# Three of the seven layer-0 chunks computed as three rounded passes, and layer-0 work placed sooner in a group

## What is computed

```
x = x0
for k in (k0, k1, k2):
    x = jnp.einsum('bhd,bmd,ohm->bod', x, x0, k)
    outputs.append(jnp.sum(x, axis=-1))
```

## Time and profile before

| what | value |
|---|---|
| median of 3 runs | 709.17 us |
| profiled execution | 707.73 us, span of its instructions 705.9 us |
| first group's first matmul | 38.57 us |
| last group's first matmul | 602.08 us |
| end of the last group's layer-1 matmuls | 636.02 us |
| distance between the first matmuls of two neighbouring groups | 36.86 us for the first, then 37.61 to 37.63 us |
| TensorE / VectorE / ScalarE / GpSimd busy, share of the span | 93% / 82% / 78% / 48% |
| mean granted TensorE clock | 0.985 of full speed |

### The profile page before, as it was taken

One profiled execution on the slowest core, in us unless ns is written; L12 is line 12 of the kernel. 1 busy time (PEld: TensorE's weight loads), 2 busy tenths in 40 slices (PEclk: granted clock), 3 DMA queues, 4 the chain that ended last, 5 costly groups with the idle time before them and its releaser, 6 DMA issues.

```text
span 705.9 us, 10117 instructions
## 1 busy us (share of the span) xinstructions
PE 658.9 (93%) x2528; PEld 467.6 (66%) x2528; DVE 581.7 (82%) x1316; ACT 550.7 (78%) x1957; POOL 336.5 (48%) x351
## 2 busy tenths in 40 slices
PE   0799999999999999999999999999999999997998
PEld 0367676767677777767676767676777777672583
DVE  0568989898998989898989898988989898997390
ACT  1268888888888888888888888888888888995393
POOL 6665747556474737373837465564737330000000
PEclk9999999999999999999999999999999999996799
DMA  6530712030303030302112030303030300200000
GB/s 211 129 115 11 262 25 101 11 114 7 118 5 120 4 116 8 97 28 70 55 40 84 11 113 11 114 6 119 5 120 4 115 7 1 78 1 0 0 1 0
DMA packets 56666, 43.04 MB, mean 61 GB/s; under 512 B 37007, under 2 KB 40335, under 8 KB 56352
## 3 DMA queue, kind: packets, MB, share of 16 engines
q1 hardware_dynamic: 50090, 40.28, 18.3%
q0 software_dynamic: 5120, 1.32, 1.9%
q10 hardware_dynamic: 1398, 0.80, 0.4%
HBM read 40.41 MB, written 1.97 MB: 60 GB/s over the span
## 4 chain that ended last, share of the span: by engine, by line
PE 74%; DVE 12%; ACT 8%; issue 2%; DMA 2%; POOL 1%; SPq 0%; ACTq 0%; DVEq 0%
PE Y L437 16%; PE Y L435 16%; PE Y L436 16%; PE X L392 13%; ACT Y L265 6%; DVE chain L338 5%; PE GB L401 4%; DVE chain L332 3%; DVE z L305 1%; PE X L466 1%; PE X L464 1%; PE X L465 1%; PE X L388 1%; POOL x0g L184 1%; ACT x1hi L229 1%
## 5 line engine op out<-in xcount | busy, mean ns | idle before, releaser
L265 ACT ACTIVATE Y<-Y,xtok 128x128 f32<-128x128 f32 x1536 | 420.6, 382 | 56.0 <-PE Y L437 56.0
L435 PE MATMUL Y<-k1lo,x1hi 128*128 128x512 f32 x640 | 305.9, 478 | 10.8 <-DVE x1lo L302 10.4
L338 DVE TENSOR_TENSOR chain<-chain,Y 128x512 f32<-128x512 f32 x384 | 263.6, 686 | 49.9 <-ACT Y L265 40.9
L437 PE MATMUL Y<-k1hi,x1lo 128*128 128x512 f32 x640 | 251.8, 393 | 0.0
L436 PE MATMUL Y<-k1hi,x1hi 128*128 128x512 f32 x640 | 250.7, 392 | 0.0
L184 POOL DMA_INDIRECT x0g<-in_table,rows_now x160 | 153.9, 962 | 42.1 <-issue 37.2
L435 PEld LDWEIGHTS Y<-k1lo,x1hi 128*128 128x128 f32 x640 | 120.3, 188 | 65.5 <-DVE x1lo L302 17.7
L205 POOL TENSOR_TENSOR diag<-xtok,mask 128x320 f32<-128x320 f32 x64 | 47.3, 740 | 230.0 <-PE GB L401 214.5
L436 PEld LDWEIGHTS Y<-k1hi,x1hi 128*128 128x128 f32 x640 | 120.7, 189 | 46.1 <-issue 21.6
L197 POOL TENSOR_TENSOR pairs<-pairs,A 120x512 f32<-120x512 f32 x105 | 133.0, 1290 | 13.6 <-DMA pairs<-scratch 12.6
L437 PEld LDWEIGHTS Y<-k1hi,x1lo 128*128 128x128 f32 x640 | 120.2, 188 | 26.2
(11 more groups left out here) (52 smaller groups left out, 262.4 us busy)
## 6 DMA issues: line engine op xcount, KB each, us to landing
pairs<-scratch SPq DMA_DIRECT2D x109, 240.0 KB
A<-scratch SPq DMA_DIRECT2D x16, 240.0 KB
k1raw<-in_k SPq DMA_DIRECT2D x1, 2560.0 KB, 9.9
x0g<-in_table,rows_now POOLq DMA_INDIRECT x160, 2.3
k2s<-in_k SPq DMA_DIRECT2D x1, 2560.0 KB, 14.2
scratch<-x0g SPq DMA_DIRECT2D x93, 20.0 KB, 1.7
pairs<-in_w SPq DMA_DIRECT2D x3, 256.0 KB, 3.0
pairs<-scratch ACTq DMA_DIRECT2D x3, 240.0 KB
```

What stands on the lines that cost most here:

```text
L265: ins = nc.scalar.activation(first[:, o] if c == 0 else y[:, o], y[:, o], ACT.Copy, scale=xtok[g % 2][:, j, m:m + 1])
L338: nc.vector.tensor_tensor(chain[:, :], chain[:, :], Y[(NCH * T + c) % YB][:, :], ALU.add).then_inc(s_chain, 1)
L435: nc.tensor.matmul(y, hi[:, tok], k1lo[:, cols], start=True, stop=False)
L437: nc.tensor.matmul(y, lo[:, tok], k1hi[:, cols], start=False, stop=True).then_inc(s_y, 1)
```

## The change

Chunks 4, 5 and 6 of layer 0 are no longer one f32 matmul each but three `f32r` passes: low weights by high products, high by high, high by low. For it ScalarE writes the high part of each product (`high_product`, a copy into the new tile `pairs_hi`), and GpSimd the low part, in place of the product (`low_product`, a subtraction). ScalarE does chunk 4's, 5's and 6's high part after its own work at p = 16, 18 and 24; GpSimd does the three low parts in tile 2, behind product 6 and ahead of that tile's four gathers. The weights are split once at the start. The matmuls of layer 0 stand at p = 5, 8, 12, 17, 23, 26, 29 in place of 5, 9, 14, 18, 22, 27, 31; `x1_high` at p = 30 in place of 33; the transposes at p = 2 in place of 1. VectorE does `x1_low` and `z0_sums` earlier in its last tile.

```diff
-XTOK_PE_AT, XTOK_AT = 1, 3
-L0_AT = (5, 9, 14, 18, 22, 27, 31)
-X1HI_AT = 33
+XTOK_PE_AT, XTOK_AT = 2, 3
+L0_AT = (5, 8, 12, 17, 23, 26, 29)
+SPLIT = (4, 5, 6)
+HIGH_AT = (16, 18, 24)
+X1HI_AT = 30
+LOWS_OF_TILE = ((), (), SPLIT, ())
...
+            def low_product(g, c):
+                pool.wait_ge(s_ph, len(SPLIT) * (g - 1) + SPLIT.index(c) + 1)
+                nc.gpsimd.tensor_tensor(pairs_lo[c][0:PR, :], pairs[c][0:PR, :], pairs_hi[c][0:PR, :].bitcast(f32),
+                                        ALU.subtract).then_inc(s_pl, 1)
...
                         for c in PRODUCTS_OF_TILE[j]:
                             product(g + 1, c)
+                        for c in LOWS_OF_TILE[j]:
+                            low_product(g + 1, c)
                     if g + 2 < NG:
                         gather(g % 2, range(*GATHERS_OF_TILE[j]))
...
+            def high_product(g, c):
+                act.wait_ge(s_prod, NC0 * (g - 1) + c + 1)
+                act.wait_ge(s_l0, NC0 * (g - 1) + c + 1)
+                nc.scalar.activation(pairs_hi[c][0:PR, :], pairs[c][0:PR, :], ACT.Copy).then_inc(s_ph, 1)
...
+                        elif p in HIGH_AT:
+                            high_product(g + 1, SPLIT[HIGH_AT.index(p)])
...
+            act.wait_ge(s_w0sum, 1)
+            nc.scalar.activation(w0hi[:, :], w0[:, SPLIT[0] * O:], ACT.Copy).then_inc(s_w0hi, 1)
...
+            dve.wait_ge(s_w0hi, 1)
+            nc.vector.tensor_tensor(w0lo[:, :], w0[:, SPLIT[0] * O:], w0hi[:, :].bitcast(f32),
+                                    ALU.subtract).then_inc(s_w0lo, 1)
...
                 add_scaled(T, 1)
+                if j == TPG - 1 and g + 1 < NG:
+                    x1_low(g + 1)
...
                 mac(T, 6)
                 if j == TPG - 1 and g + 1 < NG:
-                    x1_low(g + 1)
+                    z0_sums(g + 1)
...
                 add_scaled(T, 7)
-                if j == TPG - 1 and g + 1 < NG:
-                    z0_sums(g + 1)
...
+            def layer0_split(c):
+                i = SPLIT.index(c)
+                w, hi, lo = slice(i * O, (i + 1) * O), pairs_hi[c][0:PR, :], pairs_lo[c][0:PR, :]
+                nc.tensor.matmul(X1[:, :], w0lo[:, w], hi, start=False, stop=False)
+                nc.tensor.matmul(X1[:, :], w0hi[:, w], hi, start=False, stop=False)
+                nc.tensor.matmul(X1[:, :], w0hi[:, w], lo, start=False, stop=(c == NC0 - 1)).then_inc(s_l0, 1)
...
+                            if c0 in SPLIT:
+                                pe.wait_ge(s_w0lo, 1)
+                                pe.wait_ge(s_pl, len(SPLIT) * g + SPLIT.index(c0) + 1)
+                                layer0_split(c0)
+                            else:
+                                pe.wait_ge(s_prod, NC0 * g + c0 + 1)
+                                layer0(c0)
```

More of the change, by code:

```diff
@@ L70, in build @@
         pairs = [sb(f"pairs{i}", [P, GROUP]) for i in range(NC0)]
+        pairs_hi = {c: sb(f"pairs_hi{c}", [P, GROUP], f32r) for c in SPLIT}
+        pairs_lo = {c: over(f"pairs{c}", f"pairs_lo{c}", [P, GROUP], f32r) for c in SPLIT}
         x1hi = [sb(f"x1hi{i}", [P, GROUP], f32r) for i in range(2)]
@@ L83, in build @@
         w0 = sb("w0", [PR, NC0 * O])
+        w0hi = sb("w0hi", [PR, len(SPLIT) * O], f32r)
+        w0lo = sb("w0lo", [PR, len(SPLIT) * O], f32r)
         w2s = sb("w2s", [P, H1 // P, H2])
@@ L113, in build @@
         s_roll = [sem(f"rolled_in{i}") for i in range(NC0)]
+        s_w0hi, s_w0lo, s_ph, s_pl = [sem(n) for n in (
+            "w0hi_ready", "w0lo_ready", "high_products_ready", "low_products_ready")]
         s_first, s_prod, s_l0 = sem("first_products_ready"), sem("products_ready"), sem("l0_done")
@@ L445, in _ @@
                                 pe.wait_ge(s_xtok, g + 2)
-                            pe.wait_ge(s_prod, NC0 * g + L0_AT.index(p) + 1)
-                            layer0(L0_AT.index(p))
+                            c0 = L0_AT.index(p)
+                            if c0 in SPLIT:
[5 more added lines that the diff above has]
+                                layer0(c0)
                     if c == G_AT and T > 0:
```

## The result

The changed kernel takes 731.59 us, the median of 5 runs (725.5 to 735.96), against 708.82 for the kernel before: a ratio of 1.0328, with an interval of 1.0279 to 1.0378. It is slower by 3.3%. The forecast was 731, with 712 to 749 for 8 in 10. The profile is of the fastest of the five, 725.5 us.

A forecast was written before the change was run, and what follows sets the result against it. TensorE, busy 93%, was taken to bound the old kernel, VectorE 4 us behind. Fourteen turns of a new 39.3 us loop start the last group at 624.0, span 728.3, giving 731 us; 712 to 749 for 8 in 10.

The forecast's parts named there:

- The passes save 0.18 each: TensorE, layer 0: three passes at 0.687 us replace an f32 matmul at 0.87, saving 0.55 us per group over three chunks.
- The boundary waits go, a wait for VectorE comes, 36.8 per group without the loop: Group start: 1.38 us of TensorE waits vanish, VectorE's late reduction adds 1.1 to 35.7, giving 36.8 us per group.
- tile 3 has no layer-0 matmul: VectorE's last tile: without layer-0 work there, TensorE reaches the next `make_G` at p = 4 before VectorE delivers the reduction.
- GpSimd's low parts cost 1.27: GpSimd: three subtractions shaped like a product, 1.27 us each (bounds 1.0 and 1.6), 3.8 us more per group.
- The gathers wait for ScalarE's high part, and a loop of 39.3 us closes: GpSimd, tile 2: gathers behind `low_product` 6 wait for ScalarE behind p = 24; first product to first product takes 39.3 us.
- From the issue of the load of `A3` to the first product, 5.4: Last term of the loop: from SyncE issuing the `A3` load to the next group's first GpSimd product, 5.4 us.
- the lower bound of 4.15: Same loop term at its shortest: `A3` and the first roll, 481 KB, moved 4.15 us after the issue; loop 38.0 us.
- Waits of about 2 at the transposes and 1 at chunk 4: Sign in the profile: TensorE waits about 2 us at the transposes for `A3`, about 1 at chunk 4's passes for GpSimd.
- The sum: First product at 41.31, fourteen turns of 39.3, last group at 624.0, span 728.3: 731 us.
- The clock falls: Rival: TensorE's waits near each group's start drop the clock to 1.2 GHz; 748 us, longer stretches more; chance 0.08.
- Faster: Rival: the loop never decides, TensorE and VectorE set 36.8 us per group; 697 us, chance 0.12.
- the shorter loop: Rival: DMAs seen complete nearly with their last byte and a light subtraction, loop 38.0 us; about 713 us, chance 0.12.

The follow-up runs named there:

- e12: Kernel before with only the split of chunks 4 to 6, low parts spread, other TensorE and VectorE steps at their old places: 702.43 us, ratio 0.9902.
- e5: Changed kernel with high copies after p = 11, 16, 20 and the low parts spread over tiles 1 and 2: 700.29 us, ratio 0.9896 to the kernel before.
- e9: Changed kernel with spread low parts, earlier high copies, layer 0's last two chunks after p = 28 and 31, X1 copy after 32: 692.24 us.
- e6: Changed kernel with spread low parts, earlier high copies, only layer 0's last chunk moved to p = 31, X1 copy after 32: 700.02 us.
- e1: Changed kernel with the low parts of chunks 5 and 6 behind tile 2's four gathers, chunk 4's ahead: 707.37 us, ratio 0.9967 to the kernel before.
- e3: Changed kernel with ScalarE's high copy of chunk 6 after p = 20 instead of 24: 701.95 us, ratio 0.989 to the kernel before.
- e7: Changed kernel with one more GpSimd product per group in tile 2, ahead of the low parts: 752.07 us, ratio 1.063 to the kernel before.
- e8: Changed kernel with one more GpSimd product in tile 3, behind the gathers, outside the loop: 737.46 us, ratio 1.0424 to the kernel before.
- e11: The changed kernel itself, measured again in another set: 736.76 us, ratio 1.0405 to the kernel before.
- e10: Repeat of the changed kernel with one more GpSimd product in tile 3, outside the loop: 737.79 us, ratio 1.042 to the kernel before.
- e2: Changed kernel with all three low parts behind the four gathers of tile 2: 729.58 us, ratio 1.0286 to the kernel before.
- e4: Kernel before with only the new positions of layer 0, transposes, `x1_high`, `x1_low` and `z0_sums`, no split: 703.19 us, ratio 0.9914.

## Why the prediction was right, step by step

- *The passes save 0.18 each.* Right: 0.69 to the next chunk against 0.87, and e12 alone shows 0.46 per group, where three times 0.18 would be 0.55.
- *The boundary waits go, a wait for VectorE comes, 36.8 per group without the loop.* Right in its result: 36.9 in e5. Of the reason one half held and one did not. That ScalarE behind p = 26 to 28 holds VectorE is borne out by e9, where one chunk less ahead of p = 27 takes 0.47 us off a group. The place of TensorE's wait was wrong: the prediction has it at `make_G` at p = 4, 0.9 us; it stands at p = 1, where TensorE needs a bank that VectorE has not read yet (0.89 of e5's step), and only 0.1 is left at p = 4. The prediction's other statement, that tile 3 has no layer-0 matmul, was what e6 was built on, and e6 failed.
- *GpSimd's low parts cost 1.27.* They take 1.286, the same as a product.
- *The gathers wait for ScalarE's high part, and a loop of 39.3 us closes.* Right: the wait is in the trace (37.8 us in all), the turn is 39.43. That it causes the loss, and not the added work, is shown by e1 and e3. That it is closed is shown by e7 against e8: the same instruction costs 14.6 us more inside the loop than outside.
- *From the issue of the load of `A3` to the first product, 5.4.* 5.25 on average, 4.74 at the least and 6.82 at the most; the lower bound of 4.15 was never reached. By the packets in the trace, 480 KB, which is `A3` and the first roll, had been moved 4.1 to 4.3 us after the issue in all fourteen turns, and the product started 0.6 to 2.6 us after that. This agrees with what the Trainium skill says in "DMA: Bandwidth & Descriptors", section "Anatomy of one DMA": the semaphore comes a good while after the data. That section is headed as the path of DMAs that GpSimd issues, and this load is issued by SyncE, so the prediction carried its rule over.
- *Waits of about 2 at the transposes and 1 at chunk 4.* 17.1 us in 14 waits, 1.2 each, after a wait of 0.74 for VectorE just before; and 10.0 in 13, 0.8 each.
- *The sum.* Three terms were off, and they partly cancel in the profiled execution. The first product of group 0 started at 42.68, not at 41.31, and the turns were 0.13 longer: the last group started at 627.09, forecast 624.0. That group took 34.45 against 33.94, the 0.5 that was forecast. The tail took 61.7 us there against 69.9, which brings the span to 723.3 where 728.3 was forecast. The other four executions have spans of 729.1 to 733.7.
- *The clock falls.* The prediction gave this 0.08 and a price for a fall in every group. In the profiled execution it fell in one group of sixteen, the one of 40.81 us, after the wait of 2.05 us; in e11 once, in e10 twice, in e7 four times. So the rival is real but rare, and it lengthens single groups. It came up only in kernels whose loop is closed and, once, in e2's group 0, behind its wait of 5.83 us; between the groups of the kernel before, e1, e3 to e6, e8, e9 and e12 the profiles have none. Faster, and the shorter loop, did not come about.
- *How far a hit within 1 us is luck.* e11 tells: 736.8 for the same kernel in another set. Of the profiled execution's parts the last group's start was 3.1 us late and the tail 8.2 us short.

What stays open: why the first product of group 0 came 0.4 to 1.7 us later in every profiled execution with a new kernel (41.7 to 43.0) than in that of the kernel before. It is late in e4 too, which has no new instruction ahead of it. The delay is there before the stores to scratch: SyncE waited for the ten gathers of group 1 and began the stores at 32.15 before, and at 32.5 to 33.7 in the others. Why those gathers landed later is not shown. Also open is what decides whether the clock falls at a wait of 2 to 3 us: it did around waits of 1.79 and 2.44 us in e7 and behind 2.05 us in the changed kernel, and did not behind 2.91 us in e8.

## What to carry to other kernels

In these traces GpSimd's queue is served in order, so a small instruction that waits for another engine delays all that stands behind it: the four gathers need nothing of ScalarE, and still started 1.44 us after the low part that had waited for it 2.31 us. On the engine that issues gathers, ask of each added wait which DMA is behind it, how many microseconds of reserve that DMA chain has, and whether the work that ends the chain comes back to the instruction that waits. If it does, add up the whole loop: engines at 54% to 90% busy say nothing of it. Put work that feeds a long DMA chain first, and short work that has reserve behind it, and write down both first and later iterations, since the first has another phase.

## What the runs showed of the hardware

The tail's clock differs from one execution to the next. In the profiled executions of both kernels TensorE waits 4.15 us for VectorE at the tail's start. Before, the clock was then at 0.51 for twenty microseconds. After, it was at 0.61 of full speed in the 4 us around the end of the wait and at 0.99 in the twenty behind, and the tail was 8 us shorter, 61.7 against 69.9. The profiles of e1 and e5 lie between, with tails of 66.5; the other runs' tails took 69.9 to 71.2. The stretches of the changed kernel, and the wait:

```profile
665.00:669.00 4.00, 3.31 (x5) 1.38 (x6) 3.97 (x7) 1.94 (x5) 0.00 (x0) 0.61 0.01 2
669.00:689.00 20.00, 20.00 (x62) 10.89 (x62) 12.71 (x20) 10.68 (x19) 0.00 (x0) 0.99 0.00 1
```

```profile
665.70 1.33 PE L433 MATMUL GB<-diag,x 128*128 128x328 f32 x2 [4.16 <-DVE x L396]
```

This fits the spread of the kernel before (700.5 to 710.6 us in 17 executions beside e12, where the mean granted clock is 0.998 in the fastest and 0.983 to 0.986 in those above 708), and it means that a difference of 8 us between two single executions of these kernels need not come from the groups. And DMAs on the path bring their own spread with them: as long as they were hidden the groups repeated within 0.03 us; on the path, within 2.1, a part of which is the clock's one fall.
